# Packed queries of an attention kernel: through DRAM in five DMAs, or from SBUF to SBUF in twelve

## What is computed

```python
xn = layernorm(x)
q, k, v = split(xn @ Wqkv.T)             # 16 heads of 16 features; q is scaled by 1/4
k, v = k[::8], v[::8]                    # within each segment of 512: 64 keys
scores = q @ k.T                         # per head and segment, 512 x 64
c = max(scores over 64 queries)          # one maximum per block of 64 queries and key
w = exp(scores - c); den = sum(w) + 1e-10
att = (w @ v) / den
out = x + att @ Wout.T + (relu(xn @ W1 + b1) @ W2 + b2)      # 1024 hidden features
```

## Time and profile before

| | |
|---|---|
| median of three runs | 1117.35 us |
| the profiled execution's own time | 1118.02 us |
| its span | 1116.2 us |
| granted TensorE clock, mean | 0.988 |
| busy: TensorE / VectorE / ScalarE / GpSimd | 1080.2 / 784.9 / 648.5 / 619.5 us |
| DMA traffic | 169.36 MB, share of the 16 engines 56.4% |
| HBM read / written | 67.77 / 42.47 MB |

### The profile page before, as it was taken

One profiled execution on the slowest core, in us unless ns is written; L12 is line 12 of the kernel. 1 busy time (PEld: TensorE's weight loads), 2 busy tenths in 40 slices (PEclk: granted clock), 3 DMA queues, 4 the chain that ended last, 5 costly groups with the idle time before them and its releaser, 6 DMA issues.

```text
span 1116.2 us, 22636 instructions
## 1 busy us (share of the span) xinstructions
PE 1080.2 (97%) x7225; PEld 922.7 (83%) x7225; DVE 784.9 (70%) x1399; ACT 648.5 (58%) x1078; POOL 619.5 (55%) x488
## 2 busy tenths in 40 slices
PE   4889999999999999999999999999999999999997
PEld 3678888889888888988888888888988888888886
DVE  7787776767677677777768677667677768677630
ACT  4545565665566565565665556565556656655652
POOL 2335565555566565565565566565565555555554
PEclk9889999999999999999999999999999999999999
DMA  6446656565656565656565656555656555656511
GB/s 210 106 112 169 168 141 175 138 170 155 173 138 174 147 166 151 177 132 185 137 167 152 174 142 174 151 150 161 165 153 167 147 156 161 168 146 163 131 47 67
DMA packets 127898, 169.36 MB, mean 152 GB/s; under 512 B 24576, under 2 KB 78464, under 8 KB 127872
## 3 DMA queue, kind: packets, MB, share of 16 engines
q1 hardware_dynamic: 127872, 169.02, 56.4%
HBM read 67.77 MB, written 42.47 MB: 99 GB/s over the span
## 4 chain that ended last, share of the span: by engine, by line
PE 95%; DVE 1%; issue 1%; POOL 1%; SPq 0%; DMA 0%; POOLq 0%; ACT 0%; DVEq 0%
PE y_bank L810 41%; PE h_bank L810 40%; PE s_banks L867 5%; PE misc L939 3%; PE s_banks L939 2%; PE misc L810 2%; PE misc L905 0%; PE misc L888 0%; DVE w_exp L701 0%; DMA k_pack<-k_dram 0%; DVE s_max L695 0%; PE s_banks L810 0%; DVE xn_keys L647 0%; DVE w_lo L611 0%; POOL att L446 0%
## 5 line engine op out<-in xcount | busy, mean ns | idle before, releaser
L439 POOL TENSOR_TENSOR h_lo<-h_full,h_hi 128x512 fp32r<-128x512 f32 x256 | 337.5, 1319 | 441.4 <-ACT h_full L505 434.3
L511 ACT ACTIVATE w_exp<-w_exp 128x512 f32<-128x512 f32 x256 | 161.8, 632 | 239.8 <-DVE w_exp L701 239.8
L810 PE MATMUL y_bank<-w_hi,h_hi 128*128 128x256 f32 x1024 | 290.8, 284 | 1.2 <-ACT w_exp L511 1.2
L810 PE MATMUL y_bank<-w_lo,h_hi 128*128 128x256 f32 x1024 | 290.7, 284 | 0.0
L810 PE MATMUL y_bank<-w_hi,h_lo 128*128 128x256 f32 x1024 | 290.2, 283 | 0.0
L503 ACT ACTIVATE h_hi<-h_bank,b_cols 128x512 fp32r<-128x512 f32 x256 | 175.0, 684 | 95.7 <-PE h_bank L810 90.0
L810 PE MATMUL h_bank<-xt_hi,w_hi 128*128 128x512 f32 x512 | 209.2, 409 | 2.0 <-DVE q_lo L728 2.0
L695 DVE TENSOR_REDUCE s_max<-s_banks 128x8 f32<-128x512 f32 x256 | 174.7, 682 | 45.4 <-PE s_banks L867 44.9
L810 PEld LDWEIGHTS y_bank<-w_hi,h_hi 128*128 128x128 f32 x1024 | 195.3, 191 | 10.5 <-issue 1.4
L810 PEld LDWEIGHTS y_bank<-w_lo,h_hi 128*128 128x128 f32 x1024 | 195.8, 191 | 9.8
L810 PE MATMUL h_bank<-xt_lo,w_hi 128*128 128x512 f32 x512 | 203.0, 396 | 0.0
(11 more groups left out here) (93 smaller groups left out, 1598.9 us busy)
## 6 DMA issues: line engine op xcount, KB each, us to landing
q_pack<-q_hi SPq DMA_DIRECT2D x256, 128.0 KB, 2.4
x_raw<-x SPq DMA_DIRECT2D x32, 512.0 KB, 4.8
q_pack<-q_lo SPq DMA_DIRECT2D x128, 128.0 KB, 2.4
rden_rows<-rden_dram SPq DMA_DIRECT2D x128, 128.0 KB, 4.5
out<-y SPq DMA_DIRECT2D x32, 512.0 KB, 3.0
xt_dram<-z SPq DMA_DIRECT2D x116, 128.0 KB, 2.6
xt_raw<-xt_dram SPq DMA_DIRECT2D x29, 512.0 KB, 3.7
k_pack<-k_dram SPq DMA_DIRECT2D x96, 128.0 KB, 2.6
```

The source lines that it names most:

```text
L439: pool.tensor_tensor(h_part[1][:, i % HBUF], h_full[:, i % HBUF], f32(h_part[0][:, i % HBUF]), ALU.subtract).then_inc(h_lo, 1)
L511: act.activation(w_exp[:, pair], w_exp[:, pair], ACT.Exp).then_inc(w_ready, 1)
L810: mm = pe.matmul(ps, stationary[a], moving[b], start=start and c == 0 and n == 0, stop=stop and c == len(pairs) - 1 and n == 2, skip_group ...
```

## The change

q_part goes to DRAM by two writes of 512 KB, the high part as soon as q_hi is complete and the low part as soon as q_lo is. Both count on one semaphore, q_out. When both have landed, three reads of 512 KB bring hi, lo and hi into 32 partitions of q_pack each. They count on one semaphore, q_packed, and scores 0 waits for all three. The keys' three reads are issued between the writes and the wait for q_out. The sums' DMAs (two to DRAM, one back, the merge of num_den) follow in one piece. q_pack's layout now has the pair's j before its half, as k_pack has.

```diff
-        q_pack = sb("q_pack", [P, PAIRS, SEG], F32R)
+        q_pack = sb("q_pack", [P, PAIRS // 2, DH, SEG], F32R)
+        q_dram = nc.dram_tensor("q_dram", [2, PAIRS // 2, PW, DH * SEG], F32).ap()
...
-        pair_packed = [sem(f"pair_packed{j}") for j in range(PAIRS // 2)]
+        q_out = sem("q_out")
+        q_packed = sem("q_packed")
...
                 keys_to_dram(-2)
-                pack(-2, 0)
+                queries_to_dram(-2)
                 pack_keys(-2)
-                for j in range(1, PAIRS // 2):
-                    pack(-2, j)
+                pack_queries(-2)
...
-            def pack(s, j):
-
-                if j == 0:
-
-                    sp.wait_ge(q_hi, (s + 3) * DH)
-                    sp.wait_ge(q_lo, (s + 3) * DH)
+            def queries_to_dram(s):
+
+                sp.wait_ge(q_hi, (s + 3) * DH)
+                sp.dma_start(q_dram[0].rearrange("j d n -> (j d) n"),
+                             f32(q_part[0][:]).rearrange("p c n -> p (c n)")).then_inc(q_out, 16)
+                sp.wait_ge(q_lo, (s + 3) * DH)
+                sp.dma_start(q_dram[1].rearrange("j d n -> (j d) n"),
+                             f32(q_part[1][:]).rearrange("p c n -> p (c n)")).then_inc(q_out, 16)
+
+            def pack_queries(s):
+
+                sp.wait_ge(q_out, (s + 3) * 32)
                 for r, part in enumerate((0, 1, 0)):
-                    sp.dma_start(f32(q_pack[PW * r:PW * (r + 1), j::PAIRS // 2, :]),
-                                 f32(q_part[part][PW * j:PW * (j + 1)])).then_inc(pair_packed[j], 16)
+                    sp.dma_start(f32(q_pack[PW * r:PW * (r + 1)]).rearrange("d j c n -> d j (c n)"),
+                                 q_dram[part].rearrange("j d n -> d j n")).then_inc(q_packed, 16)
...
                 if norm:
                     keys_to_dram(s)
-                    pack(s, 0)
+                    queries_to_dram(s)
                     pack_keys(s)
-                    pack(s, 1)
+                    pack_queries(s)
                 if attention:
                     den_to_dram(s + 1)
-                if norm:
-                    pack(s, 2)
-                if attention:
                     den_spread(s + 1)
-                if norm:
-                    pack(s, 3)
...
             def scores(s, n):
 
                 pair = PAIR_ORDER[n]
-                if n % 2 == 0:
-                    pe.wait_ge(pair_packed[n // 2], (s + 2) * Q_PACKED)
 
                 if n == 0:
                     pe.wait_ge(num_den_ready, past((s + 1) * QUADS))
                     pe.wait_ge(k_packed, (s + 2) * K_PACKED)
+                    pe.wait_ge(q_packed, (s + 2) * Q_PACKED)
                 pe.wait_ge(s_shifted, past((s + 1) * PAIRS + n - 1))
-                pe.matmul(s_bank[n % 2], k_pack[0:PR, pair % (PAIRS // 2), pair // (PAIRS // 2)], q_pack[0:PR, pair], start=True,
+                pe.matmul(s_bank[n % 2], k_pack[0:PR, pair % (PAIRS // 2), pair // (PAIRS // 2)],
+                          q_pack[0:PR, pair % (PAIRS // 2), pair // (PAIRS // 2)], start=True,
                           stop=True).then_inc(s_psum, 1)
```

## The result

The changed kernel takes 1401.12 us (median of 4, 1396.78 to 1406.78) against 1117.78 (median of 4, 1116.86 to 1121.25): a ratio of 1.2531, with a 95% interval of 1.2476 to 1.2585. That is 283 us slower. The direction and the mechanism were forecast, the size was not: 1333 was said, and 1401 lies above the range's upper end of 1380. The profiled execution took 1406.78 us itself.

What follows compares the result with a forecast made beforehand. TensorE, busy for 97% of the span, was taken as the bound, so late packed queries add stalls: 1118.0 + 152 (30 steady steps) + 12 (first two) + 51 (clock) = 1333 us, range 1190 to 1380.

Steps and rivals of the forecast that it cites:

- Part 3: Three reads into 32 partitions each: 1.7 us fixed plus 7.25 us for 1.573 MB at 217 GB/s.
- Part 4: TensorE's clock behind each stall: 3.4 us at half speed, 1.7 us lost, x 30 = 51 us.
- What bounds, and the slack: TensorE runs without a gap in the steady part; q_lo to packed operands may take 6.97 or 7.66 us.
- Part 1: Two added 512 KB writes of q_part to DRAM, landed at 515.2, with q_lo ready at 511.76.
- Part 2: The keys' reads, issued right behind the writes at about 512.3 instead of 513.9, cost nothing.
- slow end: The three reads' upper bounds: 8.0 us of data by q_pack's rate, and 2.5 us fixed by xt_raw.
- The sums' DMAs: Their reads come behind the queries', at about 525 instead of 522, and stay covered before the inversion.
- Total: Whole kernel: 1118.0 + 152 + 12 + 51 = 1333 us.
- (a): Rival at the reads: narrow destination doesn't bind, data take 3.7 us; about 1195 us in all; chance 0.19.
- (c): Rival at scores 0: chain ends within 6.1 us of q_lo, early key waits go; 1113 us; chance 0.02.
- (d): Rival at scores 0: a chain of 7.0 to 7.7 us stays hidden, time stays 1118 us; chance 0.02.
- (b): Rival on TensorE's clock: every stall gives 10.3 us at half, 5.1 us lost; 1435 us; chance 0.07.

Runs made afterwards that it cites:

- the table above: Stall length against TensorE busy time for seven kernels with 32 stalls; with reads into partitions 0 to 63, 4.1 us stalls and 69.1 us above 1080.2.
- the pair of 64-partition kernels: Changed kernel with two 512 KB reads instead of three, packing left out: into partitions 0 to 63, 1311.38 us; into 32 to 95, 1205.35 us.
- wide reads: Changed kernel with each of the three reads spread over all 128 partitions instead of 32, packing left out: 1279.16 us, ratio 1.1445.
- the table of four: Group-by-group waits against one wait at scores 0: twelve SBUF-to-SBUF DMAs 1118 (before) and 1458; through DRAM 1130 (twelve reads) and 1401 (the change).

## Why the prediction was right in kind and short in size

The steps that failed are the sizes of two terms. Part 3 put the time from the reads' issue to the scores at 8.95 us, and it is 10.42 in the mean. Part 4 put the clock's cost at 51 us, 1.7 a stall, and it is about 70, or 2.2 a stall. The path, the wait and the order of the terms were right.

- **What bounds, and the slack: right.** TensorE had no slack of its own; the stall stands at scores 0, in each of 32 segments. The slack measured in the new trace is 7.75 us in the segment shown, against 7.66 said for such a segment, and 7.41 in the mean of the 30, against 7.32.
- **Part 1, the writes: nearly right.** 3.66 us from q_lo to q_out, 3.74 in the mean, 3.43 said.
- **Part 2, the keys moved, at no cost: nearly right.** Two of three keys' reads less gain 0.2 us a segment, and 4 us in the medians, which is within the noise.
- **Part 3, the reads: the term that was too small.** From issue to scores I had 1.7 + 7.25 = 8.95 us, and the segment shown has 10.31. The 7.25 are 1.573 MB at 217 GB/s, a rate read from 1.4 us of full share in the middle of rden_rows. Over all of the reads, 605.8 to about 614.1, the mean is 1.573 / 8.3 = 190 GB/s: a slow start (0.8 us at 189), a middle of 222 and 206, and a tail of 1.2 us at 87. That is 1.05 of the 1.36 us missed; the other 0.3 are the fixed part, 0.9 to the first byte and 1.1 from the last to the scores. In the sum the mean stall was 164 / 32 + the waits already there, some 5.3 us; measured, 7.03. The 30 later stalls came to 203 us instead of 152, and the first two added 17 instead of 12. I had the slow end as 8.0 us of data and 2.5 fixed, 10.5 together, which holds the 10.42: the bound was sound, and the value I took stood at the fast side.
- **Part 4, the clock: right in kind, 51 said, 68 to 71 measured.** I took one fall of 3.4 us that begins 1.5 us behind the stall. In the segment shown the clock is at half for 6.8 us (614.1 to 620.9) and falls before the scores start; 5.72 us of work lie in it, so 2.9 us are lost. Other segments differ, as two more stretches at half clock show:

```profile
402.60:409.20 6.60, 3.52 (x8) 2.84 (x9) 2.56 (x4) 0.63 (x1) 0.00 (x0) 0.50 0.51 163
...
443.50:453.60 10.10, 5.76 (x19) 5.00 (x20) 4.76 (x9) 2.42 (x4) 0.39 (x1) 0.50 0.48 138
```

  The work at half clock is 3.52 and 5.76 us in these, and the mean loss is 70 / 32 = 2.2 us a stall. The longer stalls are not the reason that it exceeds 1.7: the forecast had stalls of 5.1 us, and with 4.1 us each the loss was 69 us already (the table above).
- **The sums' DMAs: right,** 0.9997.
- **Total:** 215 us said over before, 283 measured by the medians and 288 by the spans of the profiled executions. Of the 73 missed by the spans, 56 are stalls and 17 the clock. The range's upper end of 1380 held the slow end of the rate and of the fixed part (23 + 26 us), but nothing for a clock that costs more than 51 us. Both terms erred the same way, and no run here says that this was more than chance.
- **Rivals.** (a), the wide rate, is refuted by the pair of 64-partition kernels. Even with wide reads the change costs 161 us (1279.16), where (a) had some 77. (c) and (d) fell with the first wait row. (b) was wrong as put: a stretch of about 10 us at half does occur, but part of it lies in the stall, and the mean loss is 2.2 us a stall and not 5.1.

What I had not weighed is the table of four: I costed the change as a chain of transfers, and the chain is a fact only because one semaphore makes scores 0 wait for all of it. With the same bytes in twelve reads and four semaphores it costs 12 us. No version through DRAM that was tried beats the kernel before; the twelve reads come nearest.

## What to carry to other kernels

When several transfers are joined into few, ask first what the first consumer then waits for: pieces that had landed under the work of the pieces before them all move ahead of it. Cost a transfer over its whole length, start and tail included, and not at the rate of its best microsecond, and look at which partitions it ends in, not only at how many. A stall of a few microseconds on TensorE costs more than its own length, by the slower matmuls behind it: here some 2.2 us for each stall of 4 us or more.

## What the runs showed of the hardware

- Narrow destinations: 206 to 222 GB/s into 32 partitions, 233 into 0 to 63, 377 into 32 to 95, 420 into all, all with 4 KB rows from DRAM.
- A write with 4 entries in its outermost dimension ran with a DMA share of 0.26 at 104 GB/s; the same bytes with 128 entries ran at 401.
- The 32 stalls cost TensorE 25 us of busy time by the lower clock at 2.1 us each, and 66 to 78 us at 4.1 us each and more.
- The first 0.8 us of reads of rows just written ran at 189 GB/s though the share was at its highest (1.24). Whether the fresh rows are the cause was not tried.
- Filler matmuls in a stall kept the granted clock at 0.992 and took 70 us off the time, without bringing any data earlier.
